# A graph network on one core: the setup's zeros and high one-hots move to other engines, the second layer's destination scores come in quarters

## The reference

```
x = layernorm(x + L0(x))   # weighted sum over incoming edges, then gates and two dense layers
x = layernorm(x + L1(x))   # attention by relation: 4 relations x 4 heads of 32
x = layernorm(x + L2(x))   # attention with self loops, 8 heads of 16, and a feed-forward net
x = layernorm(x + L3(x))   # largest message over incoming edges, then two dense layers

# L1, for each relation r:
h      = (x @ W[r]).reshape(N, 4, 32)
e      = leaky_relu(e_src(h)[src] + e_dst(h)[dst])
e_max  = max(segment_max(e where edge_type == r, dst), 0)
alpha  = exp(e - e_max[dst]) / (segment_sum(..., dst) + 1e-8)
out   += segment_sum(alpha * h[src], dst)
```

## Time and profile before

| | us |
|---|---|
| median of 3 runs | 4912.84 |
| lowest, highest | 4898.47, 4914.94 |
| the profiled execution, its own time | 4907.5 |
| its span | 4905.8 |
| VectorE busy | 3778.4 |
| GpSimd busy | 3402.5 |
| ScalarE busy | 2163.7 |
| TensorE busy | 2078.8 |

### The profile page before, as it was taken

How to read it: one execution, slowest core, us unless ns; L and a number is a source line. 1 busy time by engine, 2 the same in 40 slices (tenths; PEclk the granted TensorE clock), 3 DMA queues, 4 the chain that set the end, 5 groups by cost and what they waited for, 6 DMA issues and landing times. The chain is left out here.

```text
span 4905.8 us, 57881 instructions
## 1 busy us (share of the span) xinstructions
PE 2078.8 (42%) x11828; PEld 1171.3 (24%) x11828; DVE 3778.4 (77%) x7229; ACT 2163.7 (44%) x5606; POOL 3402.5 (69%) x2937
## 2 busy tenths in 40 slices
PE   2499998999952000000000300000000158998886
PEld 1355444444421000000000200000000035555553
DVE  9676666666547999889898868888888757777776
ACT  0243333333221877777775222222222145656553
POOL 0588888888717777777773467777777427777774
PEclk9899999999976555555555555555555579999998
DMA  9655555555534576666666356666666313333332
GB/s 401 199 104 99 99 99 99 99 99 99 116 66 136 206 270 242 240 258 251 242 247 239 93 182 216 215 215 215 215 215 215 119 44 124 124 119 117 121 115 85
DMA packets 281664, 816.70 MB, mean 166 GB/s; under 512 B 62405, under 2 KB 177621, under 8 KB 269522
## 3 DMA queue, kind: packets, MB, share of 16 engines
q1 hardware_dynamic: 99250, 506.75, 27.4%
q0 software_dynamic: 169776, 248.56, 23.7%
q10 hardware_dynamic: 12528, 60.37, 3.0%
HBM read 366.96 MB, written 448.51 MB: 166 GB/s over the span
## 5 line engine op out<-in xcount | busy, mean ns | idle before, releaser
L623 POOL DMA_INDIRECT tab<-arena x560 | 984.5, 1758 | 189.9 <-issue 142.2
L745 PE MATMUL psum<-arena 128*128 128x512 bf16 (+1 forms) x4704 | 950.9, 357 | 0.0
L1519 PE MATMUL psum<-ident,arena 128*128 128x128 f32 x15 | 3.7, 428 | 2219.0 <-DVEq L1547 2219.0
L1871 POOL DMA_INDIRECT arena<-table,arena x784 | 748.6, 955 | 242.4 <-issue 238.5
L1288 POOL DMA_INDIRECT arena<-table,arena x588 | 653.6, 1112 | 186.5 <-issue 174.0
L2360 POOL DMA_INDIRECT arena<-table,arena x622 | 621.2, 999 | 202.6 <-issue 185.3
L2446 PE MATMUL psum<-arena 128*128 128x512 bf16 x4050 | 683.0, 331 | 96.2 <-DVE arena L2479 55.0
L1335 ACT ACTIVATE arena<-arena 128x128 f32<-128x128 f32 x1680 | 505.9, 387 | 163.3 <-DVE arena L1447 160.7
L1447 DVE SCALAR_TENSOR_TENSOR arena<-arena 128x512 f32<-128x512 f32 x728 | 543.9, 747 | 12.1
L745 PEld LDWEIGHTS psum<-arena 128*128 128x128 bf16 x4704 | 434.0, 99 | 474.7 <-issue 26.5
L1519 PEld LDWEIGHTS psum<-ident,arena 128*128 128x128 f32 x15 | 2.7, 214 | 2219.5 <-DVEq L1547 2219.3
(11 more groups left out here) (412 smaller groups left out, 4664.8 us busy)
## 6 DMA issues: line engine op xcount, KB each, us to landing
rows<-arena SPq DMA_DIRECT2D x56, 3808.0 KB
arena<-seg_rows SPq DMA_DIRECT2D x112, 896.0 KB, 4.8
rows<-arena SPq DMA_DIRECT2D x56, 1008.0 KB
seg_rows<-arena ACTq DMA_DIRECT2D x28, 1792.0 KB
rows<-arena SPq DMA_DIRECT2D x56, 896.0 KB, 3.8
arena<-table,arena POOLq DMA_INDIRECT x1994, 3.0
arena<-src_lanes SPq DMA_DIRECT2D x56, 448.0 KB
tab<-arena POOLq DMA_INDIRECT x560
```

What stands on the lines that cost most here:

```text
L623: eng.indirect_dma_start(out=m.tabs[j], out_offset=bass.IndirectOffsetOnAxis(ap=idx[g][:, k:k + 1], axis=0), in_=rows[g][:, k, 0:D], in_of ...
L745: t = eng.matmul(ps[:, c, 0:w], part[n // 2 % PAIRS][:, n % 2, :], hot[n % HOTS][:, lo:lo + w], start=False, stop=False, skip_group_check= ...
L1871: eng.indirect_dma_start(out=kv[k][:, j, :], out_offset=None, in_=m.table2, in_offset=bass.IndirectOffsetOnAxis(ap=idx[k][:, j:j + 1], axi ...
```

## The change

In setup_phase:

- The 28 writes of zeros to `seg_rows` go from ScalarE's queue to SyncE's, behind the loads of x and ahead of the neutral rows. ScalarE's small loads follow the weights directly.
- The tables' zeros go from the end of ScalarE's program to the end of SyncE's, behind the store of `src_lanes` and a wait for `zeroed`.
- VectorE makes only the low one-hots. For the high ones GpSimd subtracts the high bits from 0..24 (`away`, 350 elements for each half), ScalarE takes the absolute value (`apart`) and then relu(1 - |d|), which is 1 where the distance is 0. ScalarE does this behind its small loads. TensorE waits for two semaphores instead of one.

In layer1_edges: `ed_all` arrives and is scanned in four quarters (64 scans of 196 elements), and the maximum over the four relations is two elementwise maxima (784 x 8, then 784 x 4) in place of one reduce.

```diff
# setup_phase
+        away = [A(HALF, NB) for _ in range(2)]
+        apart = [A(HALF, NB) for _ in range(2)]
...
             @block.gpsimd
+                eng.wait_ge(prep, S_PREV)
+                with eng.Fori(0, TURNS) as i:
+                    for h in range(2):
+                        eng.wait_ge(away_free[h], i + 1)
+                        eng.tensor_tensor(away[h], spread(iota[:, 0:NB], 1, [P, HALF, NB]),
+                                          spread(hi[:, bass.ds(i * BODY + h * HALF, HALF)], 2, [P, HALF, NB]), ALU.subtract).then_inc(away_made[h], 1)
                 eng.wait_ge(l_x, 32)
                 eng.wait_ge(zeroed, 16 * ZEROS)
...
             @block.sync
                 eng.wait_ge(const, 18)
+
+                eng.wait_ge(l_dst, 48)
+                with eng.Fori(0, TURNS) as i:
+                    eng.dma_start(lanes(m.seg_rows)[:, bass.ds(i * BODY, BODY), :].rearrange("p t f -> p (t f)"), zeros).then_inc(zeroed, 16)
                 eng.dma_start(m.rows1[EP:EP + 1, :], neutral[0:1, 0:R1]).then_inc(zeroed, 16)
...
                 eng.dma_start(m.src_lanes[0:T, :].rearrange("(b p) l -> p b l", p=SRCB), turned_src[0:SRCB]).then_inc(src_stored, 16)
+                eng.wait_ge(zeroed, 16 * ZEROS)
+
+                for j in range(TABS):
+                    eng.dma_start(m.tabs[j][0:NP, :].rearrange("(p r) f -> p (r f)", p=P), zeros[:, 0:NB * D]).then_inc(tabs_zeroed, 16)
                 eng.wait_ge(src_stored, 16)
+                eng.wait_ge(tabs_zeroed, 16 * TABS)
...
             @block.scalar
-                eng.wait_ge(const, 1)
-
-                eng.wait_ge(l_dst, 48)
-
-                with eng.Fori(0, TURNS) as i:
-                    eng.dma_start(lanes(m.seg_rows)[:, bass.ds(i * BODY, BODY), :].rearrange("p t f -> p (t f)"), zeros).then_inc(zeroed, 16)
...
                 eng.dma_start(m.edge_w[:, :], I["L3_gnn_Wm"][2 * D, :].partition_broadcast(P)).then_inc(l_small, 16)
 
+                for h in range(2):
+                    eng.nop().then_inc(away_free[h], 1)
+                eng.wait_ge(const, 18)
+                with eng.Fori(0, TURNS) as i:
+                    for h in range(2):
+                        eng.wait_ge(away_made[h], i + 1)
+                        eng.activation(apart[h], away[h], ACT.Abs).then_inc(away_free[h], 1)
+                        eng.wait_ge(away_free[h], i + 2)
+                        eng.wait_ge(hot_free[h], i + 1)
+                        eng.activation(hot_hi[h], apart[h], ACT.Relu, scale=-1.0, bias=m.ones[:, 0:1]).then_inc(high_made[h], 1)
+
                 eng.wait_ge(l_src, 48)
...
                 eng.wait_ge(l_small, 16 * SMALL)
-                eng.wait_ge(zeroed, 16 * ZEROS)
-
-                for j in range(TABS):
-                    eng.dma_start(m.tabs[j][0:NP, :].rearrange("(p r) f -> p (r f)", p=P), zeros[:, 0:NB * D]).then_inc(tabs_zeroed, 16)
-                eng.wait_ge(tabs_zeroed, 16 * TABS)
...
             @block.tensor
-                        eng.wait_ge(hot_made[h], 2 * i + 2)
+                        eng.wait_ge(hot_made[h], i + 1)
+                        eng.wait_ge(high_made[h], i + 1)
...
             @block.vector
                                           spread(lo[:, bass.ds(i * BODY + h * HALF, HALF)], 2, [P, HALF, P]), ALU.is_equal).then_inc(hot_made[h], 1)
-                        eng.tensor_tensor(hot_hi[h], spread(iota[:, 0:NB], 1, [P, HALF, NB]),
-                                          spread(hi[:, bass.ds(i * BODY + h * HALF, HALF)], 2, [P, HALF, NB]), ALU.is_equal).then_inc(hot_made[h], 1)
# layer1_edges
+        PARTS = 4
...
             @block.sync
-                for c in range(2):
-                    eng.dma_start(ed_all[:, c * T // 2:(c + 1) * T // 2, :], lanes(m.seg_dst)[:, c * T // 2:(c + 1) * T // 2, :]).then_inc(ed_in[c], 16)
+                for c in range(PARTS):
+                    t0, t1 = c * T // PARTS, (c + 1) * T // PARTS
+                    eng.dma_start(ed_all[:, t0:t1, :], lanes(m.seg_dst)[:, t0:t1, :]).then_inc(ed_in[c], 16)
...
             @block.vector
-                for c in range(2):
-
-                    t0, t1 = c * T // 2, (c + 1) * T // 2
+                for c in range(PARTS):
+
+                    t0, t1 = c * T // PARTS, (c + 1) * T // PARTS
                     eng.wait_ge(ed_in[c], 16)
                     if c:
-                        eng.wait_ge(ed_steps, RH)
+                        eng.wait_ge(ed_steps, RH * c)
...
-                eng.wait_ge(ed_steps, 2 * RH + 1)
-                f.then(eng.tensor_reduce(ed, ed_all.rearrange("p t (r a) -> p t a r", a=H1), AX.X, ALU.max))
+                eng.wait_ge(ed_steps, PARTS * RH + 1)
+                two = ed_all[:, :, 0:2 * H1]
+                eng.tensor_tensor(two, two, ed_all[:, :, 2 * H1:RH], ALU.max).then_inc(ed_steps, 1)
+                eng.wait_ge(ed_steps, PARTS * RH + 2)
+                f.then(eng.tensor_tensor(ed, ed_all[:, :, 0:H1], ed_all[:, :, H1:2 * H1], ALU.max))
```

More of the change, by code:

```diff
@@ L236, in setup_phase @@
         hot_free = [sem(f"hot_free{h}") for h in range(2)]
-        hot_made = [sem(f"hot_made{h}") for h in range(2)]
+        hot_made = [sem(f"low_hot_made{h}") for h in range(2)]
+        away_made = [sem(f"distances_made{h}") for h in range(2)]
+        away_free = [sem(f"distances_used{h}") for h in range(2)]
+        high_made = [sem(f"high_hot_made{h}") for h in range(2)]
         deg_done, cum_done, whole_done = sem("degrees_counted"), sem("degrees_summed"), sem("whole_spread")
@@ L1223, in layer1_edges @@
         SUM, MAX = REL * D, REL * D + RH
-        ed_in, ed_first_in = [sem(f"dst_scores_landed{c}") for c in range(2)], sem("first_scores_landed")
+        PARTS = 4
+        ed_in, ed_first_in = [sem(f"dst_scores_landed{c}") for c in range(PARTS)], sem("first_scores_landed")
         begun, ed_steps = sem("buffers_begun"), sem("dst_scores_steps")
@@ L1381, in _ @@
                         eng.tensor_tensor_scan(ed_all[:, t0:t1, k], m.keep[:, t0:t1], ed_all[:, t0:t1, k], before, ALU.mult, ALU.add).then_inc(ed_steps, 1)
-                eng.wait_ge(ed_steps, 2 * RH)
+                eng.wait_ge(ed_steps, PARTS * RH)
                 ed4 = ed_all.rearrange("p t (r a) -> p t r a", a=H1)
                 eng.tensor_tensor(ed4, ed4, spread(m.other_rel[:, :, :], 3, [P, T, REL, H1]), ALU.add).then_inc(ed_steps, 1)
-                eng.wait_ge(ed_steps, 2 * RH + 1)
-                f.then(eng.tensor_reduce(ed, ed_all.rearrange("p t (r a) -> p t a r", a=H1), AX.X, ALU.max))
+                eng.wait_ge(ed_steps, PARTS * RH + 1)
[3 more added lines that the diff above has]
+                f.then(eng.tensor_tensor(ed, ed_all[:, :, 0:H1], ed_all[:, :, H1:2 * H1], ALU.max))
                 f.then(eng.memset(rows[1][:, HALF - 1, :], 0.0))
```

## The result

The changed kernel takes 4946.56 us in the median of four runs (4925.98 to 4953.85), the kernel before 4908.61 in four of its own. The ratio is 1.008, with a 95% interval of 1.0061 to 1.0099: slower, by 38 us, where 4944 was forecast. The profiled execution is the fastest of the four, 4925.98 with a span of 4924.0, so the trace shows a change of 18 us and not of 38.

What follows compares the result with a forecast made beforehand. The prediction took the setup to be bound by VectorE's one-hots, with the zeros as floor, and layer 1's loop by GpSimd's gathers. One-hots +39, tail -2, layer 1 0 gave +37 us on 4907.5: 4944, range 4898 to 4988.

Steps and rivals of the forecast that it cites:

- Zeros, as a bound: Setup: scatters may not start before the zeros land, about 143 us after the change; met, with scatters at 189.
- ScalarE's late start: Setup: small loads stall beside the zeros, so ScalarE starts its one-hot part at about 34 us, 25.4 without a stall.
- the limit assumed: ScalarE's DMA queue in the setup: about 8 loads in flight, some 3 over it, costing 13 us.
- Alternation: Setup one-hots: VectorE's compare and GpSimd's subtraction exclude each other, 1.93 + 0.8 = 2.73 us per half turn, against 2.37.
- End of the one-hots: Setup: one-hots end at 34 + 1 + 54 x 2.73 + 1.5 = 184 us, against 145.1: +39.
- Tail: Setup after the one-hots: src_lanes and the tables' zeros end under the scatters, -2 us (0 to -4).
- Layer 1: First attention layer: VectorE ready 12 us sooner, but lost gathers cancel it; net 0 (from -7.6 to +5).
- The rival by which the gathers pass under the maxima: Layer 1: GpSimd's gathers aren't stalled by the maxima, gaining up to 7.6 us; no chance given.
- The sum: Whole kernel: +39 - 2 + 0 = +37 us on 4907.5, so 4944.
- The overlap rival: Setup: compare and subtraction overlap, half turn 1.93 us, zeros set the scatters at 143 to 145; 4893 to 4901; chance 0.15.

Runs made afterwards that it cites:

- zeros_only: Kernel before with only the queue moves of the zeros and tables' zeros; VectorE makes both one-hots, layer 1 as before: ratio 1.0008 to the kernel before.
- seven_last: Changed kernel with only the last seven of ScalarE's small loads behind its last copy; one run, only phases read: scatters start at 167.7 us.
- psum_iota: Changed setup, layer 1 as before, VectorE's low compare reading its 0..127 from PSUM instead of SBUF: ratio 0.9997 to the kernel before.
- layer1_only: Kernel before with all the layer1_edges edits and the setup as before: ratio 0.9971 to the kernel before.
- after_again: Changed kernel with no edit, traced a second time on the second set's chip: ratio 1.0038 to the kernel before.
- setup_only: Changed kernel with layer1_edges put back as before, so only the setup changes: ratio 1.0059 to the kernel before.
- psum_iota_smalls_last: Changed setup, low compare reading PSUM and ScalarE's small loads behind its last copy, layer 1 as before: ratio 0.9973 to the kernel before.
- smalls_last: Changed setup with ScalarE's 33 small loads behind its last copy, layer 1 as before: ratio 1.003 to the kernel before.

## Why the prediction was right, step by step

- *Zeros, as a bound*: right. They end near 148 instead of 143, and no scatter of the changed kernel waits for them. zeros_only shows that their move costs nothing.
- *ScalarE's late start*: the mechanism was right and its size too small in most runs. The zeros started at 19, near the 21 assumed. The part was to start at 34; it started at 38, and the other traces with the same queues have the last load accepted at 45 to 53. seven_last shows that the last seven loads are the whole stall, which fits the limit assumed. What varies is how many loads are held, not for how long: one is accepted per 3.9 us in every trace, in the changed kernel 3 of them, in zeros_only 5, in the others 7. The traces order themselves by how far ScalarE's queue has come when the zeros start: the load of lin_b is issued 2.1 us ahead of them in the first trace (last load accepted at 37.8), 1.8 in zeros_only (45.0), 0.4 to 0.8 in the other three (52.8 to 53.2). No run varies this alone, and where the first microsecond or two come from stays open.
- *Alternation*: right, and shown by psum_iota, which takes away the second SBUF input. Of the rows given for it, the cast beside the iota was no evidence: that cast reads one input and the iota none, so it shows that the two engines can hold each other up, but not through a second input. The 0.8 us taken for the subtraction was near (0.775), though no row of before priced its second input. The half turn was mis-sized: 2.52 us, not 2.73. The two alone take 1.93 and 0.775, in sum 2.70, so 0.18 of them overlap. 54 times 0.21 is 11 us too many.
- *End of the one-hots*: forecast 184, measured 176.3 = 39.4 + 54 x 2.51 + 1.4. ScalarE's start came 5 us later than forecast, and the shorter half turns gave back 12.
- *Tail*: -2 forecast; the next phase follows the last one-hot by 45.4 instead of 48.5, so -3.
- *Layer 1*: forecast 0 for the 57th gather, measured -1.3 in the first trace, about -3 in layer1_only and -1.6 for the maxima alone. The scans took 33.9 in a range of 32 to 37, the maxima 10.1 for 10. The rival by which the gathers pass under the maxima is ruled out: 6.42 and 3.16 us instead of 0.94.
- *The sum*: +37 was forecast. The trace has 28 from the setup and 1 back from layer 1, and 18 in the whole span. The median's 38 is more. A longer stall could explain it: with a first absolute value at 54.7, as in after_again, the next phase starts 43 us later than before. The three slower runs of the changed kernel have no trace, so this is argued, not shown. Against reading it too closely: on the other chips the same 43 to 44 us in the setup came with ratios worth 34 us (setup_only) and 22 us (after_again), and 13 us in psum_iota with none. The pitch was set 11 us too high and the stall 4 to 21 too low; that the sum came out within 3 us of the median is in part luck, since these two errors point opposite ways.
- *The overlap rival*: wrong as a forecast. Its half turn of 1.93, with the zeros as the bound, is what psum_iota_smalls_last brings about, and there the setup ends 8 us earlier, where this rival had 7.

## What to carry to other kernels

Work moved from VectorE to GpSimd doesn't run beside a VectorE instruction that reads two SBUF operands. Here that held for a subtraction with two SBUF inputs (2.39 us instead of 0.775) and for gathers, which read their indices there (6.42 instead of 0.94). Look for a small GpSimd instruction that takes as long as its neighbour, and put one operand of the VectorE instruction in PSUM before moving more work. An engine that has to start early shouldn't issue more small loads beside a bulk transfer than its queue takes at once, about 8 here by the prediction's estimate; issue them behind the engine's own work, as smalls_last and seven_last do. And an engine that becomes ready earlier gives back at most the stall of the one that sets the pace, less what it takes from it on the way.

## Not expected

ScalarE loads its table 28 times, once per turn ahead of the absolute value, 1.283 us each, though nothing but absolute value and relu runs between; beside half turns of 2.5 us it hides, but at 1.93 a turn has 3.86 us and ScalarE fills 1.28 + 2 x (0.49 + 0.59) = 3.4 of them, so little is left before ScalarE would be the bound. And the last small load is accepted at 37.8 to 53.2 in traces with the same queues, while everything before the stall agrees within 2 us: a lead of a microsecond or so over the bulk transfer goes with 15 us less behind it.
